# The last of eight feed-forward segments runs through all experts, between and behind the pairs of the one before; the second mixer's products stand four to a step

## What is computed

```python
x = x + 0.5 * ffn(layernorm(x))     # first half step
x = x + mixer(layernorm(x))
x = x + 0.5 * ffn(layernorm(x))     # second half step, the same weights
```

## Time and profile before

| what | value |
|---|---|
| median of three runs | 486.56 us |
| profiled execution | 483.66 us |
| its span, first to last instruction | 481.9 us |
| mean granted TensorE clock, 1 is 2.4 GHz | 0.882 |
| busy: TensorE / VectorE / GpSimd / ScalarE | 363.4 / 297.5 / 223.3 / 186.0 us |
| segment 4, first turn on TensorE | 231.96 us |
| segment 6, first turn on TensorE | 366.60 us |
| segment 7, first turn on TensorE | 420.84 us |
| first gather of segment 7 on GpSimd | 456.76 us |

### The profile page before, as it was taken

How to read it: one execution, slowest core, us unless ns; L and a number is a source line. 1 busy time by engine, 2 the same in 40 slices (tenths; PEclk the granted TensorE clock), 3 DMA queues, 4 the chain that set the end, 5 groups by cost and what they waited for, 6 DMA issues and landing times. The chain is left out here.

```text
span 481.9 us, 8829 instructions
## 1 busy us (share of the span) xinstructions
PE 363.4 (75%) x2224; PEld 289.1 (60%) x2224; DVE 297.5 (62%) x1114; ACT 186.0 (39%) x418; POOL 223.3 (46%) x232
## 2 busy tenths in 40 slices
PE   1999999989988849998699924999675983088600
PEld 1767676866768736776656724577564973087500
DVE  6837555756789582567699699996979350002222
ACT  1422333364664224655365611655422341033300
POOL 0005703720477605776273074076760777227374
PEclk9989899998999887999799976999975898589955
DMA  8932240231866574356733232634518573667522
GB/s 242 318 106 83 88 131 18 85 115 49 230 187 166 153 213 137 99 151 181 216 91 109 76 95 80 186 105 127 161 61 253 149 199 98 166 175 212 164 65 65
DMA packets 91838, 67.56 MB, mean 140 GB/s; under 512 B 7688, under 2 KB 88208, under 8 KB 91792
## 3 DMA queue, kind: packets, MB, share of 16 engines
q1 hardware_dynamic: 84624, 52.32, 38.0%
q0 software_dynamic: 7168, 14.69, 11.0%
HBM read 43.98 MB, written 23.00 MB: 139 GB/s over the span
## 5 line engine op out<-in xcount | busy, mean ns | idle before, releaser
L910 POOL DMA_INDIRECT xs<-xn,slot x112 | 110.8, 989 | 153.6 <-DVE slot L718 121.3
L922 POOL DMA_INDIRECT g<-ys,slot x112 | 111.4, 994 | 98.8 <-issue 73.8
L361 PE MATMUL ps_u<-xT,w1s 128*128 128x128 f32 x644 | 95.7, 296 | 6.1 <-ACT xT L504 4.5
L361 PEld LDWEIGHTS ps_u<-xT,w1s 128*128 128x128 f32 x644 | 87.8, 211 | 9.5 <-issue 5.0
L373 PE MATMUL ps_d<-w2s,hT 128*128 x644 | 89.3, 284 | 0.0
L520 ACT ACTIVATE hT<-ps_u 128x512 f32<-128x512 f32 x84 | 48.7, 580 | 103.0 <-PE ps_d L373 89.3
L755 DVE SCALAR_TENSOR_TENSOR x_res<-g,wk,x_res 128x128 f32<-128x128 f32 x112 | 33.5, 349 | 86.2 <-DMA g<-ys,slot 85.2
L373 PEld LDWEIGHTS ps_d<-w2s,hT 128*128 128x128 f32 x644 | 82.5, 200 | 2.4 <-issue 2.1
L425 PE MATMUL ps_u<-xm,mixT 128*128 128x512 f32 x160 | 76.9, 612 | 1.6 <-ACT xm L504 1.6
L351 PE MATMUL ps_t<-ident,xg 128*128 128x128 f32 x161 | 36.6, 309 | 39.1 <-issue 33.5
L351 PEld LDWEIGHTS ps_t<-ident,xg 128*128 128x128 f32 x161 | 21.1, 156 | 58.6 <-issue 49.0
(11 more groups left out here) (91 smaller groups left out, 305.3 us busy)
## 6 DMA issues: line engine op xcount, KB each, us to landing
w1s<-in_L_ffn_w_dram SPq DMA_DIRECT2D x161, 128.0 KB
ys<-y SPq DMA_DIRECT2D x35, 256.0 KB
xg<-xs SPq DMA_DIRECT2D x7, 768.0 KB, 5.1
xg<-xs SPq DMA_DIRECT2D x7, 704.0 KB, 7.1
xs<-zeros SPq DMA_DIRECT2D x10, 256.0 KB, 4.1
x_res<-in_L_attn_x_dram SPq DMA_DIRECT2D x4, 512.0 KB, 5.2
out_dram<-x_res SPq DMA_DIRECT2D x16, 128.0 KB
xs<-xn,slot POOLq DMA_INDIRECT x112
```

The lines of the kernel that those rows point to most:

```text
L361: i = pe.matmul(bank[:, c:c + P], w1s[:, G % NW, t, k * P:(k + 1) * P], xT[:, G % 2, t * P:(t + 1) * P], start=True, stop=True)
L910: pool.indirect_dma_start(out=xs[n % 2], out_offset=bass.IndirectOffsetOnAxis(ap=slot[:, n % RING, k, j:j + 1], axis=0), in_=xn[:, n % 2, ...
L922: pool.indirect_dma_start(out=g[:, k, j, :], out_offset=None, in_=ys[n % 2], in_offset=bass.IndirectOffsetOnAxis(ap=slot[:, n % RING, k, j ...
```

## The change

Segment 7 (`LAST`) is dense too. Sparse segments are 1 to 6: scatter, row load, weight loads, pairs, y stores, gather, rank and places of segment 7 are gone. Its norm, router and choice stay where they were; its turned tokens go into `xd`, the buffer of segment 0's. The first up product of its 16 rounds stands at step 3 of segment 6, one round at each of the steps 4 to 11, and the other eight behind the last pair. Down products of pairs and rounds now take the two banks in the order of their use (`down_uses`, `down_bank`). VectorE adds the rounds in turn, with the combine of segment 5 behind the fifth and that of segment 6 behind the fourteenth. The output of sequence 3 is stored in two parts of 256 KB, one for each half (`store_last`).

The mixer of sequence 1 has its 20 products at steps 0 to 4 of segment 3, four at each, and its result is turned at step 9 of that segment, before at step 0 of segment 4.

```diff
@@ -32,7 +32,8 @@
     NSEG = 2 * BATCH
-    NG = (NSEG - 1) * PAIRS
+    LAST = NSEG - 1
+    NG = (LAST - 1) * PAIRS
     NDENSE = 2 * E
@@ -50,23 +51,26 @@
-    ROUTER_AT = {(1, 4): 3, (2, 6): 4, (4, 4): 5, (5, 2): 6, (6, 1): 7}
-    RANK_AT = {(1, 6): 3, (2, 11): 4, (4, 6): 5, (5, 4): 6, (6, 3): 7}
+    ROUTER_AT = {(1, 4): 3, (2, 6): 4, (4, 4): 5, (5, 2): 6, (6, 1): LAST}
+    RANK_AT = {(1, 6): 3, (2, 11): 4, (4, 6): 5, (5, 4): 6}
+
+    DENSE_AT = {4: 1, 5: 1, 6: 1, 7: 1, 8: 1, 9: 1, 10: 1, 11: 1}
+    OPEN_AT = 3
     NORM2_AT = {(1, 3): 0, (3, 0): 1, (4, 1): 2, (4, 10): 3}
-    MIXED_AT = {(2, 0): 0, (4, 0): 1, (4, 9): 2, (5, 8): 3}
+    MIXED_AT = {(2, 0): 0, (3, 9): 1, (4, 9): 2, (5, 8): 3}
     UNITS_AT = {0: {(1, 3): 4, (1, 4): 3, (1, 5): 3, (1, 6): 2, (1, 7): 2, (1, 8): 2, (1, 9): 2, (1, 10): 2}}
-    UNITS_AT[1] = {(3, 0): 4, (3, 1): 2, (3, 2): 2, (3, 3): 2, (3, 4): 2, (3, 5): 2, (3, 6): 2, (3, 7): 2, (3, 8): 2}
+    UNITS_AT[1] = {(3, 0): 4, (3, 1): 4, (3, 2): 4, (3, 3): 4, (3, 4): 4}
     UNITS_AT[2] = {(4, 1): 4, (4, 2): 4, (4, 3): 4, (4, 4): 2, (4, 5): 2, (4, 6): 2, (4, 7): 2}
-    LOAD_AT = {(1, 7): 2, (2, 8): 3, (3, 9): 4, (4, 9): 5, (5, 9): 6, (6, 9): 7}
+    LOAD_AT = {(1, 7): 2, (2, 8): 3, (3, 9): 4, (4, 9): 5, (5, 9): 6}
     MOVES = [("to", 1), ("to", 2), ("to", 3), ("from", 1), ("to", 4), ("from", 2)]
-    for n in range(5, NSEG):
+    for n in range(5, LAST):
         MOVES += [("from", n - 2), ("to", n)]
-    MOVES += [("from", NSEG - 2), ("from", NSEG - 1)]
+    MOVES += [("from", LAST - 2), ("from", LAST - 1)]
@@ -78,6 +82,19 @@
         return (n - 1) * PAIRS + q
+
+    def rounds_at(n, q):
+
+        if n < LAST - 1 or q not in DENSE_AT:
+            return range(0)
+        first = NDENSE + sum(c for k, c in DENSE_AT.items() if k < q)
+        return range(first, first + DENSE_AT[q])
+
+    ROUNDS_AFTER = range(NDENSE + sum(DENSE_AT.values()), 2 * NDENSE)
+
+    def round_of(i):
+
+        return (LAST if i >= NDENSE else 0), i % NDENSE // E, i % E
...
@@ -225,20 +242,36 @@
             keys = [("dense", i, k) for i in range(NDENSE) for k in range(FH)]
-            for n in range(1, NSEG):
+            for n in range(1, LAST):
                 keys.append(("up", pair_of(n, 0)))
                     keys += [("mix", s, i) for i in units]
+                    if (n, q) == (LAST - 1, OPEN_AT):
+                        keys += [("dense", NDENSE, k) for k in range(FH)]
+                    keys += [("dense", i + 1, k) for i in rounds_at(n, q) for k in range(FH)]
+            keys += [("dense", i + 1, k) for i in ROUNDS_AFTER if i + 1 < 2 * NDENSE for k in range(FH)]
             return {key: i for i, key in enumerate(keys)}
+
+        def down_uses():
+            keys = [("dense", i) for i in range(NDENSE)]
+            for n in range(1, LAST):
+                for q in range(PAIRS):
+                    if q:
+                        keys.append(("pair", pair_of(n, q - 1)))
+                    keys += [("dense", i) for i in rounds_at(n, q)]
+                keys.append(("pair", pair_of(n, PAIRS - 1)))
+            return keys + [("dense", i) for i in ROUNDS_AFTER]
+
         def w1_loads(G):
-        turn_at, product_at = turn_uses(), product_uses()
+        turn_at, product_at, down_keys = turn_uses(), product_uses(), down_uses()
+        down_at = {key: i for i, key in enumerate(down_keys)}
         assert sum(k[0] == "mix" for k in product_at) == 2 * U * BATCH
@@ -300,6 +333,12 @@
+            def store_last():
+                for k in range(2):
+                    sp.wait_ge(s_dread, NDENSE + (k + 1) * E)
+                    w = slice(seq_of(LAST) * TPS + k * HT, seq_of(LAST) * TPS + (k + 1) * HT)
+                    sp.dma_start(out_tiles[:, w, :], x_res[:, w, :]).then_inc(s_out, 16)
+
             def store_out(n):
...
@@ -338,6 +378,17 @@
                 return ps_u[:, n % NU, :]
+
+            def down_bank(key):
+
+                n = down_at[key]
+                if n >= ND:
+                    kind, was = down_keys[n - ND]
+                    if kind == "pair":
+                        pe.wait_ge(s_yread, was + 1)
+                    else:
+                        pe.wait_ge(s_dread, was + 1)
+                return ps_d[:, n % ND, :]
@@ -364,13 +415,10 @@
                 pe.wait_ge(s_uread, product_at["up", G] + 1)
-                if G >= ND:
-                    pe.wait_ge(s_yread, G - ND + 1)
-                else:
-                    pe.wait_ge(s_dread, NDENSE)
+                bank = down_bank(("pair", G))
                 for t in range(tiles_of(G)):
                     for k in range(FH):
-                        i = pe.matmul(ps_d[:, G % ND, t * D:(t + 1) * D], hT[:, G % 2, t, k, :],
+                        i = pe.matmul(bank[:, t * D:(t + 1) * D], hT[:, G % 2, t, k, :],
                                       w2s[:, bass.ds(held[G][t], 1), k * D:(k + 1) * D],
...
@@ -495,7 +542,16 @@
                         rank(RANK_AT[n, q])
+                    if (n, q) == (LAST - 1, OPEN_AT):
+                        dense_up(NDENSE)
+                    for i in rounds_at(n, q):
+                        dense_up(i + 1)
+                        dense_down(i)
                 down(pair_of(n, PAIRS - 1))
+            for i in ROUNDS_AFTER:
+                if i + 1 < 2 * NDENSE:
+                    dense_up(i + 1)
+                dense_down(i)
...
@@ -615,7 +671,15 @@
                         gap_tanh(RANK_AT[n, q])
+                    if (n, q) == (LAST - 1, OPEN_AT):
+                        dense_gelu(NDENSE)
+                        gap_tanh(LAST)
+                    for i in rounds_at(n, q):
+                        dense_gelu(i + 1)
                 copy_y(pair_of(n, PAIRS - 1))
+            for i in ROUNDS_AFTER:
+                if i + 1 < 2 * NDENSE:
+                    dense_gelu(i + 1)
...
@@ -890,11 +954,15 @@
             combine_all(4)
-            choose(7)
-            places(7)
-            combine_all(5)
-            combine_all(6)
-            combine_all(7)
+            choose(LAST)
+            weigh(LAST)
+            weigh_all(LAST)
+            for i in range(NDENSE, 2 * NDENSE):
+                dense_add(i)
+                if i - NDENSE == 4:
+                    combine_all(5)
+                if i - NDENSE == 13:
+                    combine_all(6)
         def _(pool):
```

More of the change, by code:

```diff
@@ L321, in _ @@
                     store_out(n - 1)
[L322 to L323 removed]
+            store_out(LAST - 1)
+            store_last()
+            sp.wait_ge(s_out, 16 * (GROUPS * (BATCH - 1) + 2))
         @block.tensor
@@ L439, in dense_up @@
             def dense_up(i):
-                half, e = divmod(i, E)
+                n, half, e = round_of(i)
                 if i == 0:
@@ L447, in dense_down @@
             def dense_down(i):
-                half, e = divmod(i, E)
+                n, half, e = round_of(i)
                 pe.wait_ge(s_uread, product_at["dense", i, FH - 1] + 1)
-                if i >= ND:
-                    pe.wait_ge(s_dread, i - ND + 1)
-                elif i == 0:
+                if i == 0:
                     pe.wait_ge(s_w, 16 * FH)
+                bank = down_bank(("dense", i))
                 for j in range(HT):
                     for k in range(FH):
-                        t = pe.matmul(ps_d[:, i % ND, j * D:(j + 1) * D], hd[:, i % 2, k, j * P:(j + 1) * P],
+                        t = pe.matmul(bank[:, j * D:(j + 1) * D], hd[:, i % 2, k, j * P:(j + 1) * P],
                                       w2s[:, e, k * D:(k + 1) * D], start=(k == 0), stop=(k == FH - 1))
@@ L730, in weigh, with weigh_all @@
                 link(dve.tensor_scalar(wk[:, n % RING, 1, :], top[:, 5, :], -0.25, 0.25, ALU.mult, ALU.add))
-            def weigh_all():
-                by_e = [wk[:, 0, k, :].unsqueeze(1).broadcast_to([P, E, TPS]) for k in range(TOPK)]
+            def weigh_all(n):
+                by_e = [wk[:, n % RING, k, :].unsqueeze(1).broadcast_to([P, E, TPS]) for k in range(TOPK)]
                 dve.tensor_tensor(w_all[:, 0, :, :], chosen[:, 0, :, :], by_e[0], ALU.mult)
```

15 lines of the change are left out of this document (7 added, 8 removed).

## The result

The median of the changed kernel is 461.85 us (461.54 to 462.24, 4 runs), that of the kernel before on the same chip 486.25 us (479.3 to 487.33, 4 runs): ratio 0.957, 95% interval 0.9457 to 0.9683, faster. The prediction was 463.0. The profiled execution takes 461.72 us, with a span of 460.0 (459.4 predicted).

The account below looks back on a forecast made before the run. Bound: a single-file end through segment 7, TensorE waiting for DMA routing. New end 459.9 less 0.5 gives span 459.4, 22.5 us less; between 461.2 and 464.1, forecast 463.0 us, own range 458 to 468, 8 in 10 455 to 473.

Parts of the forecast that it names:

- Rounds and steps: Segment 6: a dense round takes 3.50 us, a pair plus a round 5.50 us, last pair ends at 427.5.
- The third mixer's steps: Two steps with four products each took 10.85 us, TensorE busy throughout; taken to show rounds and pairs interleave without loss.
- The new end: Behind segment 6's pairs, gather, TensorE's rounds and VectorE's adds run in parallel; adds end at 457.0, store at 459.9.
- the lower bound of 2.6: Final output store, last add to end: at least 2.6 us, as before for 128 KB; 2.9 was taken for 256 KB.
- Segment 6's start: Sign of being right: segment 6 starts within 2 us of 366.6; later than 370 would be wrong.
- The mixer: Second mixer, segments 3 and 4: products moved forward by four steps, 8 us, mostly off the path; 0.5 us gain taken.
- a gain of 0.5 us: Second mixer's move, between bounds of a 1.57 us gain and a 3.4 us loss.
- the bound of 3.4: Second mixer's move: loss of at most 3.4 us if segment 4's row load goes out later by four products.
- Rival A: TensorE's clock stays low during the rounds, 3.50 us more each, about 520 us with all sixteen; 3%, short dips 5%.
- Rival B: Segment 6's gather becomes the end, last data at 457.0 and the time 467 us; 11%.
- Rival C: Mixer's move costs: segment 4's row load goes out late, 3.4 us lost instead of the gain, 468 us; 7%.
- the 3.4 us above in place of the gain: Rival C's size: segment 4 and the chain up to segment 6 move by the mixer's bounding loss.

Follow-up runs that it names:

- the split combine: Changed kernel with segment 6's combine split on VectorE: two groups behind round 12, one behind 13, one behind 14; 463.33 us, ratio 0.9568.
- both other placements of the same rounds: Changed kernel with all sixteen rounds behind segment 6's pairs: 468.24 us; with all sixteen between them, two to a step: 492.09 us.
- the new order: Changed kernel with VectorE's gates 4 to 7 of the third mixer ahead of segment 5's choice and places: 456.54 us, ratio 0.9463.

## Why the prediction was right, point by point

- **Rounds and steps.** 3.50 and 5.50 us were predicted, 3.51 and 5.51 came; the last pair ends near 427.6 (427.5 predicted). The third mixer's steps were the right model for interleaving. That the times on the clock agree to 0.3 us is luck in part, and so is the span's 460.0 against 459.4: this execution began segment 3 2.6 us early and its first steps of segment 6 were 1.2 us shorter, which makes up for 2.9 us lost up to segment 4 and 0.9 from there to segment 6.
- **The new end.** The first gather at 430.89 (430.8 predicted), TensorE's end at 454.05 (453.8), VectorE's at 456.89 (457.0). From the last add to the end it took 3.1 us (2.9), but not for the reason given. The store was through 2.3 us after the last add, below the lower bound of 2.6, and the rest was GpSimd's DRAIN. The 2.6 read from the kernel before held such a rest too: its store was through at 481.1, 1.8 us after the last add, and the DRAIN ended at 481.7. So "VectorE is what ends last, 3 us behind TensorE, not GpSimd as now" holds for the adds only. GpSimd's queue still ends last, 0.5 us behind the store, and that is why the split combine brought nothing.
- **Segment 6's start.** 367.83, within the 2 us of 366.6 that were allowed, but by luck: 2.9 us lost between segments 3 and 4 met an execution that was 2.6 us early ahead of them.
- **The mixer.** This is the step that failed. "I take a gain of 0.5 us, because both TensorE and VectorE then wait for the same landing": only VectorE does (3.44 us, at 225.87), and the landing is not fixed at 233.11, which I had read from one trace. In place of the gain stands a loss of 2.9 us up to segment 4, near the bound of 3.4 that I had written down and argued away. The row load goes out 3.0 us later counted inside the trace, since two more products (not four) stand ahead of the y copy that releases it, and some smaller delays; and TensorE is held at step 9 by an expert load that I had not priced at all, with a stretch at a granted clock of 0.66 behind it (223.62 to 228.33). Some of this comes back between segments 4 and 6. By the timed runs the move costs 1.2% in the kernel before (0.7% by the medians of all runs), and nothing that can be told beside the dense last segment (0.9615 with it, 0.9592 without). Whether it does cost more in the kernel before is open: in the profile of it alone both distances add to 183.06 us, in before's to 182.99.
- **Rival A,** the low clock in the rounds, did not come: 1.00 in both stretches. **Rival B,** the late gather, did not either: the combine waits for nothing; that the gather still ends the program, by GpSimd's DRAIN, neither the forecast nor the rival had. **Rival C** came true up to segment 4, in place, in size and in its cause: the row load goes out late. On the clocks of the two traces it seems not to (225.03, 224.61 before), but the one began segment 3 2.6 us ahead of the other. The argument against it, that the y copies come in the same total TensorE time, overlooked the two products that moved ahead of them. That "the 3.4 us above in place of the gain" do not show in the total is the luck told above.

## What to carry to other kernels

Work out a new end as parallel chains, each in its engine's written order, and put a transfer chain of fixed length beside work that needs none of it: here 21 us of gather beside 26 us of rounds, and both other placements of the same rounds were slower. Follow every queue to its very end: here GpSimd's ends 10 us after its last gather is issued, later than the store, and what was saved on VectorE and in the stores behind it did not show. Work between steps also paces the loads that the steps consume; where it is taken out of them, the next load is the next wait. Time freed on one engine is worth nothing while the next instruction in its order waits for something else, so look for the next wait in order and move ahead of it what does not need it: that made a further 7 us here, half of it, by the medians, with the mixer's move, which without the new order had brought nothing that could be told. And compare two traces from a common point in each, not by their clocks.

## What the hardware showed that I had not expected

- The landing time of an indirect gather goes with what is queued around it. The last gather of segment 2 is used 7.48 us after its issue with the row load issued 1.0 us ahead of it, 5.1 to 5.5 us with the load 0.1 to 0.2 us behind it (three traces), and 3.0 to 3.3 us with the load 1.4 to 2.8 us behind it (ten traces; 222.64 to 225.87 in the changed kernel).
- GpSimd's queue ends with a DRAIN that is over 10.1 to 10.2 us after the start of the last gather's issue in all eleven traces with the dense last segment, and 6.2 to 6.3 us after it in the three without. In ten of the eleven it ends after the last store has landed, by 0.5 to 2.7 us, and the program ends with it.
- After a wait of 2.94 us TensorE's next groups ran up to twice as long (1.91 against 1.06 us), at a granted clock of 0.69. The same happens behind a router: in the changed kernel four records of a mixer product took 3.43 us at 261.39, at 0.54, against 1.88 at 266.66, at 1.00. It does not always happen: with the mixer's move alone a wait of 2.85 us is followed by groups of 1.13 and 1.06 us at 1.00.
